# Third layer's experts: from all eight for every token to tokens packed by expert

## Chip, cores and metric

The kernel runs on one core of a Trainium2 chip. The metric is the time of one execution on the device, in microseconds, the median of several runs.

## The reference

Four transformer-like layers on 2 x 1024 tokens of width 256, all in float32, each an attention or scan part and a feed-forward part with a residual. The change is in the feed-forward part of the third layer (`L2_ffn`), on all 2048 tokens, after a normalization:

```python
E, TOP_K, I, I_SH = 8, 2, 176, 352
logits = x @ gate_w.T                                   # 2048 x 8
routing_weights, selected = top_k(softmax(logits), 2)   # then divided by their sum
out = silu(x @ shared_gate.T) * (x @ shared_up.T) @ shared_down.T      # 352 hidden rows
g = einsum('nh,eih->nei', x, expert_gate)
u = einsum('nh,eih->nei', x, expert_up)
y = einsum('nei,ehi->neh', silu(g) * u, expert_down)    # 8 experts of 176 hidden rows
out = out + einsum('neh,ne->nh', y, combine)            # combine is 0 but for the two chosen
```

## The kernel before

The program is a sequence of phases; each has its own semaphores and buffers and ends in a barrier of all engines. Inside a phase every engine has an instruction stream written out by hand, with semaphore waits; nothing reorders it. The residual `core.x` (16 tiles of 128 tokens), the normalized tokens `core.h` and their transposed copy `core.hT` stay in SBUF.

`experts2` (line 2123) is one phase. It computes all eight experts for all tokens and lets the routing weights cancel the six that aren't chosen. Shared and expert rows are stacked: 1760 hidden rows in `RC2` = 14 chunks of 128. SyncE loads the router weights `wr`, then all weights at once: `wgu`, `spread32` (a 0/1 matrix that maps experts to hidden rows), `wd`. TensorE makes the logits (line 2166). VectorE makes the softmax, the two largest and their weights, split into three bfloat16 parts in `w`, which TensorE turns (line 2188). Then for each of 4 blocks of 512 tokens and each chunk: four float32 matmuls for gate and up (line 2175; the trace shows two passes for each), and one bfloat16 matmul that spreads the weights over the hidden rows (line 2200); ScalarE does silu, VectorE multiplies twice into `hid`. The down projection (line 2209) of a block follows, 14 matmuls for each tile of 128 tokens, added to `core.x` on VectorE.

The second layer's experts (`experts1`, line 1132: 32 experts, four a token) are already built in three phases, and the change borrows their form. `route1` counts tokens by expert with matmuls and a scan, and POOL scatters rows to a DRAM buffer with 64 indirect DMAs (line 1248) while TensorE works on the shared expert (lines 1159, 1167). `expert_rows1` loads groups of four experts (`wgu` 1408 KB, `wd` 704 KB, rows `xe` 512 KB) into two slots, turns the rows (line 1422), and runs gate/up (line 1430) and down (line 1438) matmuls. `combine1` gathers the results with 64 indirect DMAs (line 1497).

Of the kernel before, what the change touches and what calls it, by code (L numbers as in the profile page):

```python
# [8 lines left out]
F32 = mybir.dt.float32  # L9
BF16 = mybir.dt.bfloat16  # L10
# [2104 lines left out]
R2 = SH2 + E2 * I2  # L2115
RM2 = [min(P, R2 - c) for c in range(0, R2, P)]
RC2 = len(RM2)
TOP2 = 2
W2 = E2 + 1
PARTS2 = 3  # L2120


def experts2(core):

    nc, ps, hT, dram = core.nc, core.ps, core.hT, core.dram
    NTB = T // BANK
    with Phase(core, "e2") as ph:
        wr = ph.sb("wr", [P, KC, E2])  # L2130
        wgu, wd = ph.sb("wgu", [P, KC, 2, R2]), ph.sb("wd", [P, RC2, H])
        spread32, spread = ph.sb("spread32", [P, R2]), ph.sb("spread", [P, R2], BF16)
# [3 lines left out]
        top, w = ph.sb("top", [P, NT, 8]), ph.sb("w", [P, NT, P])  # L2136
        rest, part = ph.sb("rest", [P, NT, E2]), ph.sb("part", [P, NT, E2], BF16)
        wT = ph.sb("wT", [P, T], BF16)
        silu, hid = ph.sb("silu", [P, 2, BANK]), ph.sb("hid", [P, 2, RC2, BANK])
        (load_r, load, const, logit, ex_in, ex_r, own_dve, w_r, turned, wT_r, gu, silu_r, wsp, hid_r, down, x_added) = (  # L2140
            ph.sem(n) for n in ("load_r", "load", "const", "logit", "ex_in", "ex", "own_dve", "w", "turned", "wT", "gu", "silu", "wsp",
                                "hid", "down", "x"))
        block = ph.block()
        each = lambda v: v.unsqueeze(2).broadcast_to([P, NT, E2])

        @block.sync
        def _(sp):
            sp.dma_start(wr[:], dram["e2_wr"]).then_inc(load_r, 16)
            for dst, name in ((wgu, "e2_wgu"), (spread32, "e2_spread"), (wd, "e2_wd")):
                sp.dma_start(dst[:], dram[name]).then_inc(load, 16)  # L2150

        @block.gpsimd
        def _(pool):
            pool.memset(prob[:], 2.0).then_inc(const, 1)
            pool.memset(w[:], 0.0).then_inc(const, 1)
            pool.wait_ge(const, 2)
            pool.memset(w[:, :, 0:1], 1.0).then_inc(const, 1)
            pool.wait_ge(load, 16 * 3)
            pool.tensor_copy(spread[:], spread32[:]).then_inc(const, 1)

        @block.tensor
        def _(pe):
            pe.wait_ge(load_r, 16)
            for t in range(NT):
                for k in range(KC):
                    last = pe.matmul(ps[:, 7, t * E2:(t + 1) * E2], hT[:, k, t * P:(t + 1) * P], wr[:, k, :], start=(k == 0),
                                     stop=(k == KC - 1))
            last.then_inc(logit, 1)

# [1555 lines left out]
```

## Time and profile before

| what | value |
|---|---|
| median of three runs | 4460.46 us (4452.94 to 4465.13) |
| the profiled execution | 4451.35 us, span 4449.6 us |
| TensorE busy | 3893.6 us, 88% of the span |
| VectorE, ScalarE, POOL busy | 52%, 39%, 28% |
| this stage, first load to the next norm | 2177.99 to 2504.66, 326.7 us |
| the second layer's experts, three phases | 1367 to about 1770 |

Times in the rows are microseconds from the start of the span. A timeline row has start, length, engine, line, operation, what it writes and reads, and in brackets the idle time before it with what ended it. SPq is SyncE's queue, PEld TensorE's weight loads. The granted clock (PEclk) is a share of TensorE's full speed: 0.5 is 1.2 GHz, 1.0 is 2.4 GHz.

### The profile page before, as it was taken

To read this page: it belongs to the slowest core of one execution; us is meant where nothing else is said; L and a number is where in the kernel's file an instruction comes from. 1 tells how busy PE (TensorE), PEld (TensorE's weight loads), DVE (VectorE), ACT (ScalarE), POOL (GpSimd) and SP (SyncE) were. 2 spreads that over 40 slices of the span, in tenths; PEclk is the share of its full clock that TensorE was granted. 3 is DMA by queue.
4 is the path that set the end of the run, shared out by engine and by line. 5 is a ranking of instruction groups with operands and counts; after the bars stand their busy time and mean duration, and the time that the engine had idled before them with its cause. 6 is when DMAs were issued, how large, how long until landed. Compare 5 with 4: busy or idle time off the path is not lost. (4 is left out here: it accounts for less than half of the span.)

```text
span 4449.6 us, 105359 instructions
## 1 busy us (share of the span) xinstructions
PE 3893.6 (88%) x45357; PEld 2419.6 (54%) x45424; DVE 2324.5 (52%) x4313; ACT 1724.7 (39%) x2719; POOL 1224.0 (28%) x1771
## 2 busy tenths in 40 slices
PE   6888769999995686799899769999999999999879
PEld 3333555555543373477655546665666665666646
DVE  4764244454456124444433247777667777677642
ACT  2345212122112010455211145656655566655532
POOL 2000120000002405321000045555554555554512
PEclk9999759999996797899899889999999999999889
DMA  1000000000003062100100000000000000000000
GB/s 51 1 1 1 30 0 27 11 1 11 11 1 110 31 191 68 41 1 1 58 0 1 6 11 9 9 9 11 10 10 9 10 9 9 9 9 9 6 15 20
DMA packets 39404, 92.00 MB, mean 21 GB/s; under 512 B 7534, under 2 KB 27791, under 8 KB 35562
## 3 DMA queue, kind: packets, MB, share of 16 engines
q1 hardware_dynamic: 28586, 69.54, 4.7%
q0 software_dynamic: 6144, 11.62, 0.9%
q8 instruction: 361, 5.91, 0.6%
q10 hardware_dynamic: 4224, 4.19, 0.3%
q14 instruction: 89, 0.73, 0.1%
HBM read 70.05 MB, written 20.45 MB: 20 GB/s over the span
## 5 line engine op out<-in xcount | busy, mean ns | idle before, releaser
L2713 PE MATMUL ps<-h_normT,h_w 128*128 128x512 f32 (+1 forms) x1008 | 423.7, 525 | 27.3 <-DVE h_xx L3300 20.3
L3234 DVE SCALAR_TENSOR_TENSOR h_cv<-h_raw,h_cw,h_cv 128x1023 f32<-128x1023 f32 (+2 forms) x288 | 391.8, 1370 | 19.7 <-ACT h_cv L3061 18.7
L3378 DVE SCALAR_TENSOR_TENSOR h_st<-h_st,d_gcs,ps 128x64 f32<-128x64 f32 x448 | 123.4, 276 | 341.9 <-PE ps L3009 341.8
L3060 ACT ACTIVATE h_raw<-ps 128x512 f32<-128x512 f32 x192 | 114.1, 594 | 401.1 <-PE ps L2713 400.3
L2713 PEld LDWEIGHTS ps<-h_normT,h_w 128*128 128x128 f32 x1008 | 164.9, 189 | 132.3 <-issue 114.6
L460 ACT ACTIVATE a_prob<-ps 128x1024 f32<-128x1024 f32 (+1 forms) x192 | 154.6, 811 | 192.7 <-PE ps L372 104.4
L944 PE MATMUL ps<-a_probT,a_v 128*128 128x512 f32 x512 | 227.8, 604 | 0.9 <-DVE a_probT L1082 0.9
L2610 POOL TENSOR_TENSOR h_gm<-h_gm,h_tmp 128x15 f32<-128x15 f32 (+7 forms) x480 | 214.7, 447 | 37.6
L2175 PE MATMUL ps<-h_normT,e_wgu 128*128 128x512 f32 (+1 forms) x448 | 203.3, 597 | 3.6 <-DMA e_wd<-in_e_wd 2.4
L1231 POOL MEMSET r_zero<- 128x2048 f32 x1 | 1.8, 1805 | 727.5 <-POOLq L54 727.5
L3009 PEld LDWEIGHTS ps<-h_st,h_mT 64*64 64x64 f32 x1792 | 90.0, 132 | 198.3 <-issue 194.1
L548 DVE TENSOR_REDUCE a_mx<-ps 128x1 f32<-128x512 f32 (+3 forms) x288 | 145.1, 549 | 70.4 <-PE ps L301 45.7
L1039 ACT ACTIVATE a_prob<-ps,a_nbias 128x1024 f32<-128x1024 f32 x64 | 71.3, 1114 | 284.5 <-DVE a_nbias L1092 284.5
L2609 POOL TENSOR_TENSOR h_tmp<-h_gm 128x15 f32<-128x15 f32 (+7 forms) x480 | 162.2, 338 | 58.6 <-DVE h_gm L3287 23.5
L2618 POOL TENSOR_TENSOR h_xT<-h_xx,d_const 32x512 f32<-32x512 f32 x64 | 66.3, 1036 | 398.6 <-DVE h_xx L3323 396.2
L2783 PE MATMUL ps<-h_wo,h_o 128*128 128x256 f32 x512 | 163.3, 434 | 6.0 <-DVE h_o L3306 3.6
L944 PEld LDWEIGHTS ps<-a_probT,a_v 128*128 128x128 f32 x512 | 98.7, 193 | 125.1 <-issue 123.9
L136 PE MATMUL ps<-ident,h_norm 128*128 128x128 f32 x256 | 45.3, 358 | 135.8 <-DVE h_norm L115 135.8
L3013 PE MATMUL ps<-h_pT,h_st 64*64 64x64 f32 x1920 | 162.0, 245 | 1.9 <-issue 1.9
L1082 DVE COPY a_probT<-ps 128x512 f32<-128x512 f32 x128 | 82.5, 685 | 154.7 <-PE ps L994 154.7
L3009 PE MATMUL ps<-h_st,h_mT 64*64 64x64 f32 x1792 | 149.3, 242 | 7.9 <-DVE h_st L3378 4.1
L2995 PE MATMUL ps<-h_ka,h_u 64*64 64x64 f32 x2048 | 144.3, 222 | 2.9 <-issue 2.8
(537 smaller groups left out, 9334.0 us busy)
## 6 DMA issues: line engine op xcount, KB each, us to landing
m_wgu<-in_m_wgu SPq DMA_DIRECT2D x8, 1408.0 KB
h_w<-in_d_w SPq DMA_DIRECT2D x48, 128.0 KB
m_wd<-in_m_wd SPq DMA_DIRECT2D x8, 704.0 KB
m_rows_in<-r_zero SPq DMA_DIRECT2D x4, 1024.0 KB
e_xe<-m_rows_in SPq DMA_DIRECT2D x8, 512.0 KB
m_rows_out<-e_y ACTq DMA_DIRECT2D x8, 512.0 KB
e_wgu<-in_e_wgu SPq DMA_DIRECT2D x1, 3520.0 KB
a_t_raw<-in_t_w SPq DMA_DIRECT2D x4, 768.0 KB
```

The source lines that it names most:

```text
L460: act.activation(prob[:, u % 3, :, c0:BANK], ps[:, SB0 + 2 * g:SB0 + 2 * g + 2, c0:BANK], ACT.Exp, scale=1.0 / float(np.sqrt(D0))).then_in ...
L548: dve.tensor_reduce(mx[:, b * NQ + qt, part, m:m + 1], ps[:, bank(), 0:k1 - k0], AX.X, ALU.max).then_inc(freed, 1)
L944: last = pe.matmul(ps[:, 6 + m, :], v[:, b * NQ + kt, m * P:(m + 1) * P], probT[:, blk % 2, kt, :], start=(kt == 0), stop=(kt == NQ - 1))
L2175: last = pe.matmul(ps[0:m, 3 * (n % 2) + s, :], wgu[:, k, s, c * P:c * P + m], hT[:, k, tok], start=(k == 0), stop=(k == KC - 1))
L2609: c.link(pool.tensor_tensor(part, column, row, ALU.mult))
L2610: c.link(pool.tensor_tensor(target, target, part, ALU.subtract))
L2713: last = pe.matmul(ps[:, PROJ[m], lo:hi], w[:, kind, k, :], hT[:, k, b * S + tb * BANK + lo:b * S + tb * BANK + hi], start=(k == 0), stop= ...
L2783: last = pe.matmul(ps[:, POUT[k], j * H:(j + 1) * H], o[:, tile * P:(tile + 1) * P], wo[:], start=True, stop=True)
L2995: last = pe.matmul(res(h, c), u_[rows(own), c, :], ka[b][rows(own), c, 1, :], start=True, stop=(c == 0), tile_position=(64 * own, 64 * (1 ...
L3009: last = pe.matmul(ps[rows(h), D3 + c % 2, 0:HALF], mT[rows(h), c, :], st[rows(h), c, :], start=False, stop=True, tile_position=(64 * h, 6 ...
L3013: last = pe.matmul(res(h, c), st[rows(h), c, :], pT[rows(h), c, :], start=False, stop=True, tile_position=(64 * h, 64 * (1 - h)))
L3234: dve.scalar_tensor_tensor(out=d, in0=raw[:, kind, 0:S - back], scalar=tap(pr, kind, TAPS3 - 1 - back), in1=d, op0=ALU.mult, op1=ALU.add). ...
```

## The change

`experts2` becomes three phases, and the expert part runs only for chosen pairs of token and expert.

`route2`: VectorE computes, for each of the two choices of every token, the row of a DRAM buffer that it goes to. The buffer is packed by expert, each expert's part rounded up to tiles of 128 rows; 39 tiles (`TILES2`) are the most that 4096 pairs can need, and all 39 are always run. VectorE also computes the expert of each tile (`eid`). SyncE zeroes the buffer (5.1 MB, four DMAs), POOL scatters the rows with 32 indirect DMAs, and the other engines do two of the four token blocks of the shared expert.

`expert_rows2`: for each tile SyncE reads its expert's number from SBUF into a register and loads the rows and that expert's weights by register address, into a ring of four slots. A round of TensorE turns the rows of one tile, multiplies the next older one by gate and up, turns the hidden rows of the one before that, and projects down the oldest.

`combine2`: POOL gathers 32 times, VectorE adds the rows with their weights, and the other two blocks of the shared expert run. Weights are laid out by expert on the host side.

```diff
+TILES2 = TOP2 * NT + E2 - 1
 def experts2(core):
+        route2(core, rows_in, wv, idx, eid, sgu, sd)
+        expert_rows2(core, rows_in, rows_out, eid)
+        combine2(core, rows_out, wv, idx, sgu, sd)
...
+def route2(core, rows_in, wv, idx, eid, sgu, sd):
...
-            for dst, name in ((wgu, "e2_wgu"), (spread32, "e2_spread"), (wd, "e2_wd")):
+            for dst, name in ((sgu, "e2_sgu"), (sd, "e2_sd")):
                 sp.dma_start(dst[:], dram[name]).then_inc(load, 16)
+            sp.wait_ge(zeroed, 1)
+            for i in range(4):
+                sp.dma_start(rows_in.rearrange("(p r) n -> p (r n)", p=P)[:, i * ZW:(i + 1) * ZW], zero[:]).then_inc(zero_put, 16)
...
+            for r in range(TOP2):
+                pool.wait_ge(routed, r + 1)
+                for t in range(NT):
+                    pool.indirect_dma_start(out=rows_in, out_offset=bass.IndirectOffsetOnAxis(ap=idx[:, r, t:t + 1], axis=0),
+                                            in_=core.h[:, t, :], in_offset=None, bounds_check=TILES2 * P - 1,
+                                            oob_is_err=False).then_inc(scattered, 16)
...
+            for c in range(SC2):
+                shared_up2(pe, core, 0, c, 0, sgu, gu, hid_r)
+            pe.wait_ge(mask_r, 1)
...
+            pe.matmul(ps[:, CNT, 0:NT * E2], before[:], flat, start=True, stop=True)
+            pe.matmul(ps[:, CNT, NT * E2:2 * NT * E2], core.ones[:], flat, start=True, stop=True).then_inc(counted, 1)
+            pe.wait_ge(routed, 1)
+            shared_down2(pe, core, 0, sd, hid, hid_r, down, x_added)
+            for c in range(SC2):
+                shared_up2(pe, core, 1, c, 1, sgu, gu, hid_r)
+            shared_down2(pe, core, 1, sd, hid, hid_r, down, x_added)
...
+def expert_rows2(core, rows_in, rows_out, eid):
+    WR = 4
...
+            for i in range(TILES2):
+                s = i % WR
+                e = sp.value_load(eid[0:1, i:i + 1], min_val=0, max_val=E2 - 1)
+                if i >= WR:
+                    sp.wait_ge(down, i - WR + 1)
+                sp.dma_start(x[:, s], xin[i]).then_inc(loaded[s], 16)
+                sp.dma_start(wgu[:, s], dram["e2_egu"][bass.ds(e, 1)].rearrange("o p k n -> (o p) k n")).then_inc(loaded[s], 16)
+                sp.dma_start(wd[:, s], dram["e2_ed"][bass.ds(e, 1)].rearrange("o p c n -> (o p) c n")).then_inc(loaded[s], 16)
...
+            def turn_in(i):
+                s = i % WR
+                pe.wait_ge(loaded[s], 48 * (i // WR + 1))
+                if i >= 2:
+                    pe.wait_ge(xT_r, i - 1)
+                for k in range(KC):
+                    last = pe.transpose(ps[:, XT + i % 2, k * P:(k + 1) * P], x[:, s, k * P:(k + 1) * P], core.ident[:])
+                last.then_inc(turned, 1)
+
+            def gate_up(i):
...
+                for k in range(KC):
+                    last = pe.matmul(ps[:, GU + i % 2, 0:2 * I2], xT[:, i % 2, k, :], wgu[:, i % WR, k, :], start=(k == 0), stop=(k == KC - 1))
...
+            def turn_hid(i):
...
+            def project_down(i):
...
+                for c, m in enumerate(IM2):
+                    last = pe.matmul(ps[:, Y + i % 2, 0:H], hidT[0:m, i % 2, c, :], wd[0:m, i % WR, c, :], start=(c == 0), stop=(c == IC2E - 1))
+                last.then_inc(down, 1)
+
+            turn_in(0)
+            for i in range(TILES2 + 2):
+                if i + 1 < TILES2:
+                    turn_in(i + 1)
+                if i < TILES2:
+                    gate_up(i)
+                if 0 <= i - 1 < TILES2:
+                    turn_hid(i - 1)
+                if 0 <= i - 2 < TILES2:
+                    project_down(i - 2)
...
+                    act.activation(silu[:, i % 2, :], ps[:, GU + i % 2, 0:I2], ACT.Silu).then_inc(silu_r, 1)
...
+                    act.activation(y[:, n % WR, :], ps[:, Y + n % 2, 0:H], ACT.Copy).then_inc(y_r, 1)
+                    act.wait_ge(y_r, n + 1)
+                    act.dma_start(yout[n], y[:, n % WR]).then_inc(stored[n % WR], 16)
...
+def combine2(core, rows_out, wv, idx, sgu, sd):
...
+            for t in range(NT):
+                for r in range(TOP2):
+                    pool.indirect_dma_start(out=row[:, TOP2 * t + r, :], out_offset=None, in_=rows_out,
+                                            in_offset=bass.IndirectOffsetOnAxis(ap=idx[:, r, t:t + 1], axis=0),
+                                            bounds_check=TILES2 * P - 1, oob_is_err=False).then_inc(fetched[t], 16)
...
+            inner(0, 0)
+            add_rows(0)
+            inner(0, 1)
+            add_rows(1)
...
```

SyncE's queue in this stage before: the whole of its work is four loads at the start. (`e_wgu` and `e_wd` hold all 1760 rows.)

```order
91 L2146 UNCONDITIONAL_BRANCH [waits barrier_Pool_Activation_PE_DVE_SP_release]
92 L2148 DMA e_wr<-in_e_wr 128x16
93 L2150 DMA e_wgu<-in_e_wgu 128x7040
94 L2150 DMA e_spread<-in_e_spread 128x1760
95 L2150 DMA e_wd<-in_e_wd 128x3584
```

The same queue now, in the phase of the tiles, at tiles 3 and 4. Semaphores are named by their number's first user in the program; `a0_smax` is `down` here. TENSOR_LOAD reads the expert's number, ISA rows compute addresses.

```order
120 L2358 TENSOR_LOAD e_eid
121 L2358 ISA x2
122 L2361 DMA g_x<-e_rows_in 128x256
123 L2362 ISA
124 L2362 DMA g_wgu<-in_e_egu 128x704
125 L2363 ISA
126 L2363 DMA g_wd<-in_e_ed 128x512
127 L2358 TENSOR_LOAD e_eid
128 L2358 ISA x2
129 L2361 DMA g_x<-e_rows_in 128x256 [waits a0_smax]
```

From tile 4 on the first of the three DMAs waits for `down`, and the other two are queued behind it.

TensorE before, after the weights are turned: chunk after chunk, each waiting only for a buffer freed two chunks earlier.

```order
2825 L2175 MATMUL ps<-h_normT,e_wgu 128x512 [waits a0_vproj]
2826 L2175 MATMUL ps<-h_normT,e_wgu 128x512 x3
2827 L2200 MATMUL ps<-e_wT,e_spread 128x512
2828 L2175 MATMUL ps<-h_normT,e_wgu 128x512 [waits a0_vproj]
2829 L2175 MATMUL ps<-h_normT,e_wgu 128x512 x3
```

TensorE now, from turn_in(3) in round 2 to turn_in(4) in round 3. Line 2373 is turn_in, 2381 gate_up, 2389 turn_hid, 2397 project_down. `ln0_rstd` stands for `loaded[3]`, `init_loaded` for `loaded[0]`.

```order
2846 L2373 MATMUL ps<-ident,g_x 128x128 [waits a0_qr,ln0_rstd]
2847 L2373 MATMUL ps<-ident,g_x 128x128
2848 L2381 MATMUL ps<-g_wgu,g_xT 128x352 [waits a0_kzd,a0_qr]
2849 L2381 MATMUL ps<-g_wgu,g_xT 128x352
2850 L2389 MATMUL ps<-ident,g_hid 128x128 [waits a0_kzd]
2851 L2389 MATMUL ps<-ident,g_hid 48x128
2852 L2397 MATMUL ps<-g_wd,g_hidT 128x256 [waits a0_vd]
2853 L2397 MATMUL ps<-g_wd,g_hidT 128x256
2854 L2373 MATMUL ps<-ident,g_x 128x128 [waits a0_qr,init_loaded]
```

The second row of line 2397 is the one that counts up `down`; the row behind it is the first that needs the slot's next load.

## Rows read from the trace of the kernel before

**Rows 1.** The page, part 1: busy time, share of the span, instructions

```profile
PE 3893.6 (88%) x45357; PEld 2419.6 (54%) x45424; DVE 2324.5 (52%) x4313; ACT 1724.7 (39%) x2719; POOL 1224.0 (28%) x1771
```

**Rows 2.** Windows of the stage: length, busy by engine, PEclk, DMA share, GB/s

```profile
2178.00:2196.00 18.00, 13.82 (x64) 13.73 (x64) 1.85 (x12) 2.88 (x3) 2.18 (x3) 0.54 0.87 353
2196.00:2304.00 108.00, 105.88 (x262) 47.20 (x268) 43.78 (x113) 18.19 (x31) 1.65 (x1) 0.98 0.00 0
2304.00:2504.00 200.00, 199.06 (x696) 129.96 (x700) 46.88 (x74) 17.31 (x29) 0.00 (x0) 1.00 0.00 1
```

**Rows 3.** Timeline of all engines at the stage's edges

```profile
2177.99 0.33 SPq L2148 DMA_DIRECT2D e_wr<-in_e_wr  x1
...
2179.78 13.82 PE L2166 MATMUL ps<-e_wr,h_normT 128*128 128x8 f32 x64 [3.16 <-DMA e_wr<-in_e_wr]
...
2196.05 8.99 PE L2175 MATMUL ps<-h_normT,e_wgu 128*128 128x512 f32 x16 [2.44 <-DMA e_wd<-in_e_wd]
...
2201.65 0.60 ACT L2223 ACTIVATE e_silu<-ps 128x512 f32<-128x512 f32 x1 [5.74 <-PE ps L2175]
...
2504.66 5.33 DVE L107 BATCH_NORM_STATS2 ln_stats<-x_resid 128x6 f32<-128x256 f32 x16 [0.82 <-PEq L54]
```

**Rows 4.** Timeline of the second layer's routing, from the counts to the first scatter

```profile
1413.95 3.34 DVE L1343 TENSOR_TENSOR r_offs<-ps,r_offs 128x32 f32<-128x32 f32 x15
...
1421.41 0.17 DVE L1356 CAST r_sidx<-r_got 128x16 int32<-128x16 f32 x1
...
1422.62 1.23 POOL L1248 DMA_INDIRECT m_rows_in<-h_norm,r_sidx  x1 [41.16 <-issue]
```

**Rows 5.** Line 1248 (the 64 scatters): ns min/median/max, first and last start

```profile
L1248 POOL DMA_INDIRECT m_rows_in<-h_norm,r_sidx x64: 971/976/1226, 1422.6 to 1504.7; - x64
```

**Rows 6.** Timeline of SyncE's loads in the second layer's expert phase

```profile
1543.36 1.12 SPq L1404 DMA_DIRECT2D e_xe<-m_rows_in  x2
1561.14 0.36 SPq L1409 DMA_DIRECT2D m_wgu<-in_m_wgu  x1
...
1562.21 0.38 SPq L1411 DMA_DIRECT2D e_xe<-m_rows_in  x1
...
1588.66 0.34 SPq L1409 DMA_DIRECT2D m_wgu<-in_m_wgu  x1
```

**Rows 7.** Timeline of TensorE in the same phase

```profile
1547.47 1.76 PE L1422 MATMUL ps<-ident,e_xe 128*128 128x128 f32 x7 [6.19 <-DMA e_xe<-m_rows_in]
...
1569.25 3.62 PE L1438 MATMUL ps<-m_wd,e_hid 88*128 88x256 f32 x16
1575.22 1.97 PE L1422 MATMUL ps<-ident,e_xe 128*128 128x128 f32 x8 [2.35 <-DMA e_xe<-m_rows_in]
...
1584.88 3.62 PE L1438 MATMUL ps<-m_wd,e_hid 88*128 88x256 f32 x16
1588.34 1.04 PE L1422 MATMUL ps<-ident,e_xe 128*128 128x128 f32 x8
```

**Rows 8.** Windows of the same phase's start: length, busy by engine, PEclk, DMA share, GB/s

```profile
1544.00:1547.50 3.50, 0.03 (x1) 0.03 (x1) 0.00 (x0) 0.00 (x0) 0.00 (x0) 0.57 0.80 249
1547.50:1551.00 3.50, 3.50 (x16) 3.17 (x17) 1.39 (x2) 0.00 (x0) 0.00 (x0) 0.50 0.17 55
1551.00:1561.00 10.00, 10.00 (x76) 9.53 (x76) 1.68 (x4) 1.52 (x4) 0.00 (x0) 0.99 0.00 0
```

**Rows 9.** Timeline of TensorE under and after the second layer's last scatters

```profile
1507.76 1.01 PE L1159 MATMUL ps<-h_normT,m_sgu 128*128 128x512 f32 x1 [1.79 <-issue]
1510.55 17.33 PE L1159 MATMUL ps<-h_normT,m_sgu 128*128 128x512 f32 x36 [1.78 <-issue]
```

**Rows 10.** Timeline between the second layer's expert and combine phases

```profile
1652.56 1.02 ACT L1456 ACTIVATE e_y<-ps 128x1024 f32<-128x1024 f32 x1 [3.08 <-PE ps L1438]
...
1657.64 22.41 PE L1159 MATMUL ps<-h_normT,m_sgu 128*128 128x512 f32 x48 [5.12 <-PEq L54]
...
1659.78 1.01 POOL L1497 DMA_INDIRECT c_row<-m_rows_out,m_gidx  x1 [0.30 <-issue]
```

More of the change, by code:

```diff
@@ new lines, in shared_up2, with shared_down2 @@
+def shared_up2(pe, core, b, c, tb, sgu, gu, hid_r):
+    n, m = b * SC2 + c, SM2[c]
+    if n >= 3:
+        pe.wait_ge(hid_r, n - 2)
+    for s in range(2):
+        for k in range(KC):
+            last = pe.matmul(core.ps[0:m, 2 * (n % 3) + s, :], sgu[:, k, s, c * P:c * P + m], core.hT[:, k, tb * BANK:(tb + 1) * BANK],
+                             start=(k == 0), stop=(k == KC - 1))
+    last.then_inc(gu, 1)
+def shared_down2(pe, core, b, sd, hid, hid_r, down, x_added):
+    pe.wait_ge(hid_r, (b + 1) * SC2)
+    for j in range(4):
+        if b >= 1 and j % 2 == 0:
+            pe.wait_ge(x_added, 4 * b + j - 2)
+        for c in range(SC2):
+            last = pe.matmul(core.ps[:, 6 + j // 2, (j % 2) * H:(j % 2 + 1) * H], hid[0:SM2[c], b, c, j * P:(j + 1) * P], sd[0:SM2[c], c, :],
+                             start=(c == 0), stop=(c == SC2 - 1))
+        if j % 2:
+            last.then_inc(down, 1)
@@ new lines, in _ @@
+            own.link(dve.tensor_tensor(cnt[:], cnt[:], each(two_t[:]), ALU.subtract))
+            own.link(dve.tensor_tensor(cnt[:], cnt[:], mask[:], ALU.mult))
+            dve.wait_ge(counted, 1)
+            tot = ps[:, CNT, NT * E2:2 * NT * E2].rearrange("p (t e) -> p t e", e=E2)
+            own.link(dve.memset(offs[:, 0, :], 0.0))
+            for t in range(1, NT + 1):
+                own.link(dve.tensor_tensor(offs[:, t, :], tot[:, t - 1, :], offs[:, t - 1, :], ALU.add))
+            own.link(dve.tensor_tensor(pos[:], ps[:, CNT, 0:NT * E2].rearrange("p (t e) -> p t e", e=E2), offs[:, 0:NT, :], ALU.add))
@@ new lines, in _ @@
+            own.link(dve.tensor_tensor(ex[:], ex[:], each(linv[:]), ALU.mult))
+            for r in range(TOP2):
+                chosen(wv[:, r, :], r, ex[:])
+            for b in range(2):
+                for c in range(SC2):
+                    n, m = b * SC2 + c, SM2[c]
+                    dve.wait_ge(silu_r, n + 1)
+                    dve.tensor_tensor(hid[0:m, b, c, :], ps[0:m, 2 * (n % 3) + 1, :], silu[0:m, n % 3, :], ALU.mult).then_inc(hid_r, 1)
+                for j in range(4):
+                    t = 4 * b + j
+                    dve.wait_ge(down, 2 * b + j // 2 + 1)
+                    dve.tensor_tensor(core.x[:, t, :], ps[:, 6 + j // 2, (j % 2) * H:(j % 2 + 1) * H], core.x[:, t, :],
+                                      ALU.add).then_inc(x_added, 1)
```

335 lines of the change are left out of this document (219 added, 116 removed).

## The prediction

> **What bounds the kernel now.** I read the page's first part, then the stage of the third layer's experts by stretches, then its edges in the timeline. TensorE is busy for 88% of the whole span [rows 1]; in the stage itself it is busy 105.88 of 108 us and 199.06 of 200 us in the two stretches after routing, at a granted clock of 0.98 and 1.00, while DMA moves nothing and VectorE idles more than half [rows 2]. So the stage is TensorE's own work at full clock. It begins when SyncE issues its first load at 2177.99 and ends where the next layer's norm begins at 2504.66: 326.7 us [rows 3]. Nothing else of the program is edited, so the sum is: new length of this stage minus 326.7.
>
> The edit cuts that work. Before, every token goes through 1760 hidden rows; after, through 352 shared rows and 39 tiles of 128 packed rows. If TensorE stayed the bound this would pay. The question is what the other engines and the loads do, and the second layer's experts (lines 1183 to 1536) are built the same way, so their rows price nearly every new step.
>
> **Part 1, routing (`route2`).** Logits cost what they do now: 13.8 us from 2179.78, to 2193.6 [rows 2, 3]. Then three shared chunks run. Now the first chunk of eight 512-column passes needs 5.6 us (2196.05 to 2201.65), as the clock is still low (0.54 before it) [rows 2, 3]. At full clock sixteen 256-column passes, as many columns, took 3.6 us [rows 7], 3.4 without the last one's drain. So 5.6 + 3.4 + 3.4 puts the counting matmuls at 2206.1, and 0.6 us later VectorE has its counts. The second layer's chain from there to its first index cast took from 1413.95 to 1421.58, 7.6 us on rows of 512 elements [rows 4]; here the rows have 128, and I take 5.8 us: 2212.5. The other routing arithmetic lies beside the shared chunks or beside the scatters. POOL's first scatter followed the cast by 1.2 us [rows 4]. There are 32 scatters where the second layer has 64; those 64 started between 1422.6 and 1504.7, 1.30 us apart, 0.98 us each [rows 5]: 31 x 1.30 + 0.98 = 41.3 us, ending at 2255.0. Landing costs about 1.8 us, as the 8 KB load's (2177.99 to 2179.78) [rows 3], and the phase's end 1.5 us: **2258.3, or 80.3 us**. What is left of the shared work (a down projection of 5.2 us, three chunks of 10.3, 5.2 again: 21 us) fits under the 41 us of scatters. Zeroing 5.1 MB of the row buffer is over by then: the same stretch now moves 353 GB/s for 18 us [rows 2]. One thing can break the cover: under the second layer's scatters TensorE fell to one matmul per 2.8 us until they were over, with nothing else for it to wait for (1.01 us busy, 1.79 idle by "issue" each, ending in the burst at 1510.55) [rows 9]. I add nothing here and up to 12 us in the range.
>
> **Part 2, the expert tiles (`expert_rows2`).** This decides. Follow one ring slot. SyncE loads tile i only when `down` has counted tile i-4. TensorE runs, in order: turn_in(i+1), gate_up(i), turn_hid(i-1), project_down(i-2). So project_down(0) is the last thing of round 2, and turn_in(4), which needs the load that project_down(0) has just released, is the first thing of round 3. **Four slots are held by a pipeline four deep: no load is ever ahead.** TensorE executes in order, so everything of a round is queued behind the landing, and for tiles 4 to 38, 35 times, the period is a whole load plus a whole round.
>
> *The load.* 128 x (256 + 704 + 512) x 4 bytes = 0.754 MB in three DMAs. Two landings of the second layer's experts bracket it: 0.524 MB issued at 1543.36 let TensorE start at 1547.47 (4.11 us), and 2.687 MB issued at 1561.14 at 1575.22 (14.08 us) [rows 6, 7]; 8 KB took 1.79 us [rows 3]. The line from 8 KB to either gives 4.4 and 4.6 us per MB, so 1.79 + 0.754 x 4.5 = 5.2 us. From the end of a down projection to SyncE's issue lie 0.16 us (1584.88 + 3.62 to 1588.66) [rows 6, 7]. So **5.3 us**. Bounds: at the rate of the stage's own big load, 353 GB/s [rows 2], it is 1.79 + 2.1 + 0.16 = 4.1 us; the third issue comes 1.07 us after the first (1561.14 to 1562.21) [rows 6], which gives no less than 3.8; the previous tile's 0.131 MB store in the way makes it 5.9.
>
> *The round.* Full clock: eight transposes took 1.04 us, so 2 + 2 cost at most 0.52; sixteen 256-column passes 3.62 us, so four cost 0.90 and four of 352 columns 1.24 [rows 7]. Sum 2.66 us. At low clock transposes took 1.97 us for the same eight [rows 7]; everything doubled is 5.3 us. Which clock? After TensorE's waits the clock was 0.57 (1544 to 1547.5), stayed at 0.50, which is 1.2 GHz, for the first 3.5 us of work, and was 0.99 after that [rows 8]. Each round here follows 5 us without a matmul, so it starts low: 3.5 us low, and the remaining third at full speed, 3.5 + 1.8 / 2 = 4.4, say **4.5 us**. The bounds are 2.7 (full clock throughout) and 5.3 (never back).
>
> Period 5.3 + 4.5 = **9.8 us**, 35 times: 343 us. In front stand the first four loads, 5.2 + 3 x 3.3 us (0.754 MB x 4.4), and most of a round behind them: 19 us. Behind stand three rounds without loads, about 7 us, and the last store: in the second layer 5.1 us from the end of the last down projection (1652.5) to the next phase's start at 1657.64 [rows 10]. **Together 374 us.** ScalarE's and VectorE's work, about 1.5 us a tile each, lies inside the load and costs nothing; so do SyncE's register load and two address computations per tile, since they run before `down` arrives, except for those of the second and third DMA, which are in the 1.07 us above.
>
> The Trainium skill ("DMA: Bandwidth & Descriptors", "Anatomy of one DMA") fits a transfer as 2.0 us plus bytes at 436 GB/s, measured on another issuing path. It would make the load 3.9 us and the total 49 us shorter. The second layer's two landings were slower than that, 4.4 and 4.6 us per MB against 2.3, so the sum goes by them.
>
> **Part 3, gathering (`combine2`).** 32 gathers, each 1.00 us busy and 0.30 idle as in the second layer [rows 10]: 0.8 + 41.3, then 2 us for the last landing and adds, 1.2 for the barrier: 45 us. The other half of the shared work, 31 us, runs beside it. VectorE's adds come in strict order with the shared blocks, so a starved TensorE shows here; I add 5 us: **50 us**.
>
> **Sum.** 80.3 + 374 + 50 = 504.3 us, plus 0.8 us of barriers, against 326.7: **+178 us**. The profiled execution took 4451.35 us, so 4630; it lies 9.1 us below the median of 4460.46, so against the median **4640 us**, rounded.
>
> **Rivals.**
> 1. *Same mechanism, quick landings and early clock.* Load 4.1 us, round 4.0: 35 x 1.7 = 60 us less, 4580; at the bounds of both (3.8 + 2.7) 4525. For: the queue that moved 353 GB/s. Against: both landings of tiles with 1 KB rows.
> 2. *Same mechanism, clock never back and TensorE starved.* Load 5.9, round 5.3: +49 us, plus 12 for starving: 4701. For: rounds of 5 us barely outlast the 3.5 us that the clock took to return, and rows 9.
> 3. *Faster: the ring does run ahead.* If loads streamed, the period would be the larger of TensorE's 2.66 us and the bytes: 0.885 MB in and out at the second layer's 13.1 us for 3.2 MB (1575.22 to 1588.34) [rows 7], 3.6 us. Then 35 x 6.2 = 217 us less: 4423. It decides the sign below a period of 4.7 us (9.8 - 178 / 35). Against it stands the order of the code: even the 8 KB landing (1.79 us) with a full-clock round gives 4.5 us, which only just gets there, and a tile's load is 90 times that size. The Trainium skill ("Trainium Kernel Development and Optimization", "Best Practices") says to double-buffer so that DMA overlaps compute; four slots look like twice that, and by that rule this rival would be the forecast. Whether slots run ahead depends on when they are freed, which the code order shows.
> 4. *The change doesn't cut the work:* all 39 tiles always run, and their rounds sum to 104 us at full clock against 305 now (105.88 + 199.06) [rows 2], so it does.
>
> **Chances.** Forecast with a period of 8.8 to 10.8 us: 0.72. Rival 1: 0.14. Rival 2: 0.09. Rival 3: 0.04. Something that cancels to within 0.3% (about what a measurement of this kernel can tell from no change): 0.01. Faster 0.04, same 0.01, slower 0.95. The range takes in rival 1 down to a period of 7.0 us and rival 2 whole: 4540 to 4705.
>
> **What the profile after should show.** SyncE issuing three DMAs every 9.8 us, each first one about 0.2 us after the line-2397 matmuls end; TensorE idle before line 2373, released by DMA, 35 times about 5.3 us; granted clock in these stretches between 0.5 and 0.8; DMA share near 0.3, about 90 GB/s; scatters 1.28 to 1.30 us apart. Wrong would be: TensorE's waits before line 2373 under 2 us (rival 3), or waits on ScalarE or VectorE inside a round.

## The result and the profile after

The changed kernel takes **4643.48 us** (median of four runs, 4640.71 to 4651.48), the kernel before in the same comparison 4461.24 us (4452.94 to 4465.13): ratio **1.042, 95% interval 1.040 to 1.044**, 182 us slower. The forecast was 4640 us. The profiled execution took 4644.92 us, its span is 4642.8.

TensorE's line on the page answers to [rows 1], and the one group that the change added to the page's list of the costliest points at the cause:

```profile
PE 3857.5 (83%) x45064; PEld 2393.6 (52%) x45120; DVE 2320.7 (50%) x4434; ACT 1723.5 (37%) x2749; POOL 1288.3 (28%) x1838
...
L2373 PE MATMUL ps<-ident,g_x 128*128 128x128 f32 x78 | 26.5, 442 | 172.7 <-DMA g_wd<-in_e_ed 172.7
```

TensorE's busy time fell only from 3893.6 to 3857.5 us, since much of the smaller work is done at half clock, and 172.7 us of idle time stand before line 2373, the transposes that wait for a tile's load. The edges of the three phases, from the timelines of SyncE, POOL and VectorE, answer to [rows 3]:

```profile
2177.29 0.33 SPq L2203 DMA_DIRECT2D r_wr<-in_e_wr  x1
...
2269.32 0.33 SPq L2361 DMA_DIRECT2D g_x<-e_rows_in  x1
...
2640.23 1.04 POOL L2474 DMA_INDIRECT c2m_row<-e_rows_out,e_idx  x1 [387.12 <-SPq L51]
...
2703.48 1.73 DVE L107 BATCH_NORM_STATS2 ln_stats<-x_resid 128x6 f32<-128x256 f32 x5 [0.88 <-PEq L54]
```

The last phase's first matmul stands at 2639.5, 0.7 us before the first gather. So:

| part | predicted | measured |
|---|---|---|
| routing | 80.3 | 92.0 |
| tile phase | 374 | 370.2 |
| gathering | 50 | 64.0 |
| stage | 505 | 526.2 |
| stage, before | 326.7 | 326.7 |

The stage grew by 199.5 us, the span by 193.2: what stands ahead of the stage was 0.7 us shorter and what follows it 5.6 us shorter in this execution. The medians differ by 182.2.

The windows (length, busy time of each engine, granted clock, DMA share, GB/s), to be read against [rows 2]:

```profile
2212.00:2253.00 41.00, 18.04 (x48) 10.48 (x48) 8.71 (x23) 1.19 (x2) 31.34 (x32) 0.71 0.28 100
...
2284.90:2619.40 334.50, 175.44 (x408) 96.39 (x408) 39.31 (x136) 23.82 (x69) 0.00 (x0) 0.60 0.27 90
```

In the second row's 334.5 us the ring goes round 34 times, from SyncE's fifth load to its last: 9.84 us a tile. TensorE works 175.44 us of it, 5.16 a tile, at a mean clock of 0.60, and DMA is 27% busy: **neither is a limit, they take turns.** The table of waits for that stretch (engine, line waited at, releaser: us in total, times, longest) has the other 4.68 us:

```profile
PE ps L2373 <- DMA g_wd<-in_e_ed: 159.1, 34, 5.7
```

One turn in the timeline of all engines:

```profile
2289.26 0.69 PE L2373 MATMUL ps<-ident,g_x 128*128 128x128 f32 x2 [4.43 <-DMA g_wd<-in_e_ed]
...
2289.74 2.55 PE L2381 MATMUL ps<-g_wgu,g_xT 128*128 128x352 f32 x4
...
2292.08 0.63 PE L2389 MATMUL ps<-ident,g_hid 128*128 128x128 f32 x2
...
2292.51 2.21 PE L2397 MATMUL ps<-g_wd,g_hidT 128*128 128x256 f32 x4
...
2294.75 0.33 SPq L2361 DMA_DIRECT2D g_x<-e_rows_in  x1
...
2299.30 0.69 PE L2373 MATMUL ps<-ident,g_x 128*128 128x128 f32 x2 [4.59 <-DMA g_wd<-in_e_ed]
```

The down projection ends at 2292.51 + 2.21 = 2294.72; SyncE issues the load of the tile four further on 0.03 us later; TensorE's next instruction needs just that load. Windows of one such turn show the clock (the seventh figure is PEclk):

```profile
2324.00:2325.50 1.50, 0.00 (x0) 0.00 (x0) 0.00 (x0) 0.00 (x0) 0.00 (x0) 0.99 0.92 282
2325.50:2327.70 2.20, 0.00 (x0) 0.00 (x0) 0.00 (x0) 0.00 (x0) 0.00 (x0) 0.50 0.56 197
2327.70:2329.70 2.00, 1.97 (x5) 1.48 (x6) 0.42 (x1) 0.00 (x0) 0.00 (x0) 0.50 0.00 0
2329.70:2331.70 2.00, 2.00 (x6) 0.96 (x5) 0.46 (x2) 0.32 (x1) 0.00 (x0) 0.50 0.00 0
2331.70:2333.20 1.50, 1.11 (x3) 0.44 (x2) 0.36 (x2) 0.35 (x1) 0.00 (x0) 0.80 0.02 5
```

In this turn it drops to 1.2 GHz halfway through the wait and comes back to 2.4 GHz about when the round is over. The turns are not alike. In 14 of the 34 it stays at 0.50 from the start of the round to the end of the wait, as in the turn shown before:

```profile
2289.26:2299.30 10.04, 5.46 (x12) 2.90 (x12) 1.15 (x4) 0.70 (x2) 0.00 (x0) 0.50 0.28 88
```

In the other 20 it comes back between 2.7 us into the round and the round's end. Windows laid on every round and every wait give a mean of 0.54 in the rounds and of 0.67 in the waits, so most of the little time at the higher clock goes to an idle engine.

What the sum left out lies in the two phases with indirect DMAs. In the first of the two windows, under the scatters, TensorE works only 18.04 of 41 us. ScalarE's silu steps in the routing phase (timeline, with idle time and releaser in brackets), and the matmuls behind them (`remote`: the profile names no engine of this core as releaser):

```profile
2235.03 0.60 ACT L2171 ACTIVATE r_silu<-ps 128x512 f32<-128x512 f32 x1 [29.70 <-remote]
2249.17 0.60 ACT L2171 ACTIVATE r_silu<-ps 128x512 f32<-128x512 f32 x1 [13.54 <-remote]
2257.63 0.59 ACT L2171 ACTIVATE r_silu<-ps 96x512 f32<-96x512 f32 x1 [7.86 <-remote]
...
2258.99 7.92 PE L2158 MATMUL ps<-e_sd,r_hid 128*128 128x256 f32 x24 [22.58 <-DVE r_hid L2327]
```

Such steps follow each other 3.44 us apart when nothing disturbs them (0.60 + 2.84), and the first is due near 2229.4, 3.4 us after the second block's matmuls begin at 2225.95. Here, under the scatters (32 of them, started between 2212.2 and 2252.1), it is 5.7 us late, and they stand 14.1 and 8.5 us apart, so the last down projection begins at 2259 and ends after the scatters that should have covered it. In the last phase the same happens under the gathers: its last down projection waits 18.81 us and starts at 2687.71.

### The profile page after: what moved, and what is told of

It is laid out like the page before. It is cut to its first block and busy times, and to the rows that moved or that the text cites. A ratio compares the mean times of both kernels' runs of the same rounds, so it can differ in the third digit from the quotient of the medians.

```text
span 4642.8 us, 105738 instructions
## 1 busy us (share of the span) xinstructions
PE 3857.5 (83%) x45064; PEld 2393.6 (52%) x45120; DVE 2320.7 (50%) x4434; ACT 1723.5 (37%) x2749; POOL 1288.3 (28%) x1838
## 5 line engine op out<-in xcount | busy, mean ns | idle before, releaser
L2373 PE MATMUL ps<-ident,g_x 128*128 128x128 f32 x78 | 26.5, 442 | 172.7 <-DMA g_wd<-in_e_ed 172.7
```

## Experiments

Times are medians unless one time is said, and ratios are to runs of the kernel before on the same chip. Its median there was 4453.25 us for the first four kernels and 4451.74 for the two after them, against 4461.24 in the comparison above, so a difference to the changed kernel's 4643.48 carries an uncertainty of some 10 us; the periods in the traces do not.

### One more slot, and twice the slots

The ring's size is one number, in `expert_rows2`.

```diff
-    WR = 4
+    WR = 5
```

> The changed kernel with five slots in the ring of tiles instead of four. Theory (a load is released at the end of a round and, with four slots, needed at the start of the next; with n slots the period is (load + round) / (n - 3), down to the larger of the round and the bytes): one load is ahead, the period falls from 9.84 us to (5.1 + 2.7) / 2 to (5.1 + 4.5) / 2 = 3.9 to 4.8 us, TensorE's waits before line 2373 to 1 or 2 us each, the clock back near 1.0; 35 x 5.0 to 5.9 = 175 to 207 us less than 4643, so 4436 to 4468. Rival (the loads' rate is the bound, 0.885 MB at the 90 GB/s that the stretch shows): the period stays 9.8 us and the time 4643.

Measured: 4441.63 us, ratio to the kernel before 0.998 (0.996 to 1.000). The time is in the range that was expected. From SyncE's sixth load (2283.65) to its last (2421.82) the period is 4.19 us on average, where it was 9.84. The rounds vary: most run at full clock in 2.9 us, some at a mean clock near 0.63 in 4.5 us. Timeline of TensorE:

```profile
2333.96 0.44 PE L2373 MATMUL ps<-ident,g_x 128*128 128x128 f32 x2 [1.41 <-DMA g_wd<-in_e_ed]
...
2337.10 0.44 PE L2373 MATMUL ps<-ident,g_x 128*128 128x128 f32 x2 [0.24 <-DMA g_wd<-in_e_ed]
```

```diff
-    WR = 4
+    WR = 8
```

> The changed kernel with eight slots. Theory: four loads ahead, so the period is the larger of a full-clock round, 2.7 us, and the bytes, 0.885 MB at 245 GB/s, 3.6 us; 35 x 6.2 = 217 us less than 4643, so 4426, and little better than five slots (0 to 40 us). DMA share 0.8 or more, 240 GB/s or more in the stretch. Rival (rate bound at 90 GB/s): 4643.

Measured: **4395.68 us** (4389.94 to 4398.91), ratio 0.988 (0.986 to 0.990), the fastest of all and 248 us under the changed kernel. One round of TensorE and the start of the next, and a window over the loaded part of the tile phase, from SyncE's ninth load to its last:

```profile
2301.70 0.44 PE L2373 MATMUL ps<-ident,g_x 128*128 128x128 f32 x2
2301.98 1.35 PE L2381 MATMUL ps<-g_wgu,g_xT 128*128 128x352 f32 x4
2303.16 0.38 PE L2389 MATMUL ps<-ident,g_hid 128*128 128x128 f32 x2
2303.38 1.22 PE L2397 MATMUL ps<-g_wd,g_hidT 128*128 128x256 f32 x4
2304.54 0.44 PE L2373 MATMUL ps<-ident,g_x 128*128 128x128 f32 x2
```

```profile
2283.00:2366.00 83.00, 83.00 (x354) 49.62 (x352) 33.53 (x116) 20.65 (x59) 0.00 (x0) 1.00 0.95 323
```

No bracket stands behind any row: TensorE never waits here, its clock is 1.00, and the period is its own 2.84 us. The stage took 269.9 us (2176.14 to 2446.05) against 326.7: 57 us less, and the medians differ by 57.6. So the slots are the cause, and the price of the missing one is the largest term of all. The expectation for eight slots was 30 us too high: it took 3.6 us a tile as the bytes' limit, and they fit under 2.84 us. But they only just fit: the 16 DMA engines are busy for 95% of the window, at 323 GB/s, so a shorter round of TensorE would gain little.

### The same four slots, another order

A slot is freed by the down projection of tile i-2. Here that comes first in a round instead of last, and the transposes that need the next load come last.

```diff
             turn_in(0)
             for i in range(TILES2 + 2):
-                if i + 1 < TILES2:
-                    turn_in(i + 1)
+                if 0 <= i - 2 < TILES2:
+                    project_down(i - 2)
                 if i < TILES2:
                     gate_up(i)
                 if 0 <= i - 1 < TILES2:
                     turn_hid(i - 1)
-                if 0 <= i - 2 < TILES2:
-                    project_down(i - 2)
+                if i + 1 < TILES2:
+                    turn_in(i + 1)
```

> The changed kernel with four slots, but TensorE's round in the order project_down(i-2), gate_up(i), turn_hid(i-1), turn_in(i+1): the same work, the slot is freed before gate_up and turn_hid instead of right before the wait. Theory (it is the place of the release that counts): period = down + load + turn_in = 0.9 + 5.1 + 0.3 at full clock to 1.8 + 5.1 + 0.5 at low clock, 6.3 to 7.4 us; 35 x 2.4 to 3.5 = 85 to 120 us less, so 4523 to 4558. Rival (the sum of load and round is fixed by something else): 4643.

Measured: 4457.22 us, ratio 1.002 (1.001 to 1.004); the period is 4.29 us from 2311.8 on. Four rounds before that (2279.2 to 2307.3) take 7.02 us each, with the clock at 0.50, so the mean over all loads behind the fourth is 4.59. The lowest time that was expected, 4523, was 66 us too high. Timeline of TensorE:

```profile
2330.56 1.32 PE L2397 MATMUL ps<-g_wd,g_hidT 128*128 128x256 f32 x4 [1.15 <-DVE g_hidT L2453]
...
2334.85 1.33 PE L2397 MATMUL ps<-g_wd,g_hidT 128*128 128x256 f32 x4 [1.15 <-DVE g_hidT L2453]
```

The wait for the load is gone altogether. `project_down(i-2)`, at the start of round i, frees the slot of tile i+2, which is wanted by `turn_in(i+2)`, at the end of round i+1: nearly two rounds later. The expectation had counted less than one. What comes late now is VectorE's copy of the turned hidden rows (line 2453), which the down projection follows directly, and that puts 1.15 us of idle time into each period. So 186 us can be had back without a byte of memory.

### What the clock costs

Nine float32 matmuls of 256 columns, whose result nobody reads, ahead of TensorE's wait for a load (tiles 4 to 38).

```diff
                 s = i % WR
+                if i >= WR:
+                    for f in range(9):
+                        pe.matmul(ps[:, XT + i % 2, H:2 * H], core.ident[:], core.h[:, f, :], start=True, stop=True)
                 pe.wait_ge(loaded[s], 48 * (i // WR + 1))
```

> The changed kernel with work added, none taken away: before each wait for a load (tiles 4 to 38) nine float32 matmuls of 256 columns into an unused half of a PSUM bank, 3.9 us at full clock, whose results nobody reads. Theory (the low clock in each round comes from TensorE's idle time in the load): the clock in the stretch rises from 0.60 to near 1.0, the round falls from 4.5 to 2.7 us, period 5.1 + 2.7 = 7.8 to 8.0 us; 35 x 1.9 = 65 us less, 4578, though there is more work. Rival (the round is long for another reason, as latencies between the engines): the period stays at 9.8 or grows.

Measured: 4561.06 us, 82 us *less* than the changed kernel with 145 us more work (35 x 4.15) on the same engine. Timeline of TensorE:

```profile
2330.39 4.15 PE L2371 MATMUL ps<-h_norm,ident 128*128 128x256 f32 x18
2335.09 0.44 PE L2376 MATMUL ps<-ident,g_x 128*128 128x128 f32 x2 [0.55 <-DMA g_wd<-in_e_ed]
2335.36 1.35 PE L2384 MATMUL ps<-g_wgu,g_xT 128*128 128x352 f32 x4
```

Line 2384 is the old 2381: 1.35 us instead of 2.55, and the clock stays at 1.00. The period is 7.56 us on average over the 34 (SyncE's fifth load at 2292.58, its last at 2549.49) instead of 9.84, so the low clock costs 2.3 us a round; the load stays in the path, 4.15 + 0.55 = 4.7 us in the rows shown.

### What the weights' part of the load costs

Here the weights are loaded for the first four tiles only, and later tiles take what lies in their slot; only the rows are loaded anew, and TensorE waits for that one DMA (its changed wait is not shown).

```diff
+                if i >= WR:
+                    continue
                 sp.dma_start(wgu[:, s], dram["e2_egu"][bass.ds(e, 1)]...).then_inc(loaded[s], 16)
                 sp.dma_start(wd[:, s], dram["e2_ed"][bass.ds(e, 1)]...).then_inc(loaded[s], 16)
```

> The changed kernel, but the expert weights are loaded for the first four tiles only; from tile 4 on SyncE loads just the packed rows, so the later tiles multiply by stale weights. Load 0.131 MB instead of 0.754 MB, one DMA instead of three. Theory (load = 1.8 us + 4.5 us per MB): load 1.8 + 0.6 + 0.16 = 2.5 us instead of 5.1; round 2.7 to 4.5 us as the clock goes; period 5.2 to 7.0 us, so 100 to 162 us less than 4643: 4481 to 4543. Rival (a fixed cost makes the load, not its bytes): load 4.5 us or more, 4620.

Measured: 4538.67 us, ratio 1.017 (1.008 to 1.027), within the range that was expected. Timeline of TensorE (line 2375 is the old 2373):

```profile
2305.82 0.44 PE L2375 MATMUL ps<-ident,g_x 128*128 128x128 f32 x2 [2.04 <-DMA g_x<-e_rows_in]
```

With 0.131 MB instead of 0.754 the wait is 2.0 us instead of 4.7: 2.7 us for 0.623 MB, 4.3 us per MB, near what the two landings of the second layer had. That isn't bytes alone, for two DMAs went with them, and the last of three is issued 1.03 us after the first (2284.86 and 2285.89 in the profile after); how the 2.7 us divide is not shown. A load of a sixth of the bytes, put in the path, still leaves the kernel slower than before. **What decides is the turn-taking; the bytes set what a turn costs.**

### Why the shared blocks fall behind under the indirect DMAs

POOL waits until the shared blocks are done before it scatters.

```diff
             pool.wait_ge(zero_put, 16 * 4)
+            pool.wait_ge(x_added, 8)
```

> The changed kernel, with POOL's 32 scatters held back until the two shared blocks of the routing phase have been added. Theory (it is POOL's indirect DMAs that starve the other engines: ScalarE's gaps of 13 us before line 2171, VectorE's before line 2327, TensorE's 22.6 us): without scatters beside them the shared blocks end near 2243 instead of 2267, no gap over 3 us before these lines; the scatters then take 41 us alone, the phase ends near 2286 instead of 2269, +17 us: 4660. Rival (the gaps belong to the shared block's own waits): they stay, the phase ends near 2310, +40 us: 4683.

Measured: 4676.01 us, ratio 1.048 (1.038 to 1.058). With no scatter beside them, ScalarE's steps stand in their row (timeline):

```profile
2237.15 0.60 ACT L2171 ACTIVATE r_silu<-ps 128x512 f32<-128x512 f32 x1 [23.14 <-PE ps L2146]
2240.58 0.60 ACT L2171 ACTIVATE r_silu<-ps 128x512 f32<-128x512 f32 x1 [2.84 <-PE ps L2146]
```

In the kernel of the section above, on the same chip, they are late as in the changed kernel (2233.43, 2246.78, 2255.92). So the indirect DMAs are what delays them. But giving up the overlap costs more than the delay: the routing phase takes 114.6 us (SyncE at 2184.55 and 2299.19) against 92.0, 23 us more where 17 were expected. The rest of the 33 us between the medians is not from the edit alone, since in the profiled execution the stage begins 7.3 us later and what follows it is 9.6 us longer than in the changed kernel's, while the other two phases are 8 us shorter; the cause of these is not shown.

To see what is late, instructions or semaphores, runs that wait for nothing inside were put beside these late scatters: 80 activations, 60 reductions on VectorE, 40 matmuls of 512 columns.

```diff
+            act.wait_ge(x_added, 8)
+            for n in range(80):
+                act.activation(pa[:, n, :], core.hT[:, 0, (n % 8) * 256:(n % 8 + 1) * 256], ACT.Silu)
```

> The kernel with the scatters held back until the routing phase's shared blocks are added, and, beside the scatters, work added whose results nobody reads: 80 silu of 256 columns on ScalarE (0.4 us each), 60 reductions of 512 elements on VectorE (0.7 us), 40 float32 matmuls of 512 columns on TensorE (0.86 us each in two passes), each engine's in one run with no semaphore between them. Theory A (under POOL's indirect DMAs the other engines get their instructions late): gaps of 1 us and more without a semaphore appear inside these runs on one or more engines, and they take longer than 32, 42 and 34 us. Theory B (it is the semaphores that arrive late): the runs go through without gaps, and only work that waits for another engine is slow.

Measured: 4689.66 us (one time). Timelines of ScalarE, VectorE and TensorE; rows without gaps between instructions are drawn together:

```profile
2243.90 16.36 ACT L2267 ACTIVATE r_pa<-h_normT 128x256 f32<-128x256 f32 x53 [7.06 <-DVE x_resid L2339]
...
2263.28 0.42 ACT L2267 ACTIVATE r_pa<-h_normT 128x256 f32<-128x256 f32 x1 [1.01 <-issue]
```

```profile
2243.79 35.68 DVE L2342 TENSOR_REDUCE r_pd<-h_normT 128x1 f32<-128x512 f32 x60
```

```profile
2243.92 28.59 PE L2258 MATMUL ps<-h_norm,ident 128*128 128x512 f32 x66 [0.84 <-DVE x_resid L2339]
...
2282.23 1.01 PE L2258 MATMUL ps<-h_norm,ident 128*128 128x512 f32 x1 [1.79 <-issue]
```

No semaphore stands between these instructions, and still ScalarE comes to start one only every 1.40 us and TensorE one pass every 2.80, the spacing of [rows 9], until the scatters are over; then both run without gaps. So it is not semaphores that are late in these runs, but the instructions; why they are is not shown. The second probe asks whether the first 53, 60 and 66 are a number or a time, with 160, 200 and 120 shorter ones (here VectorE's, against the first probe):

```diff
-            for n in range(60):
-                dve.tensor_reduce(pd[:, n:n + 1], core.hT[:, 0, 0:BANK], AX.X, ALU.max)
+            for n in range(200):
+                dve.tensor_reduce(pd[:, n:n + 1], core.hT[:, 0, 0:P], AX.X, ALU.max)
```

> As the kernel with the late scatters, with longer runs of shorter instructions beside them, none of which waits for anything inside its run: 160 silu of 64 columns on ScalarE, 200 reductions of 128 elements on VectorE, 120 matmuls of 128 columns (240 passes) on TensorE. In the first probe ScalarE ran 53 activations in 16.4 us without a gap and then one every 1.40 us until the scatters were over; TensorE ran 66 passes in 28.6 us and then one every 2.80 us; VectorE's 60 had no gap at all (35.7 us). Theory A (count: an engine has some 50 to 66 instructions at hand when the scatters start, and what comes after arrives late): ScalarE's first gap comes after about 53 again, so after some 8 us instead of 16; TensorE's after about 66 passes, some 10 us; VectorE, spared before because its run was short, falls into gaps as well after some 60, about 10 us after its start, and its 200 take until the scatters end. Theory B (time: it takes 16 and 28 us of scatters until the engines are hit): gaps begin at the same times as before, after far more instructions, most of them done by then. Theory C (VectorE is exempt): its 200 show no gap while the others do. The whole program comes out near 4690 to 4700 us, as the first probe did.

Measured: 4691.84 us (one time). Timelines of ScalarE, VectorE and TensorE:

```profile
2243.58 7.59 ACT L2267 ACTIVATE r_pa<-h_normT 128x64 f32<-128x64 f32 x51 [7.06 <-DVE x_resid L2339]
2251.55 0.40 ACT L2267 ACTIVATE r_pa<-h_normT 128x64 f32<-128x64 f32 x2 [0.38 <-issue]
```

```profile
2243.47 11.68 DVE L2342 TENSOR_REDUCE r_pd<-h_normT 128x1 f32<-128x128 f32 x60
2255.83 0.48 DVE L2342 TENSOR_REDUCE r_pd<-h_normT 128x1 f32<-128x128 f32 x2 [0.68 <-issue]
```

```profile
2243.60 7.19 PE L2258 MATMUL ps<-h_norm,ident 128*128 128x128 f32 x62 [0.85 <-DVE x_resid L2339]
2251.55 0.40 PE L2258 MATMUL ps<-h_norm,ident 128*128 128x128 f32 x2 [0.76 <-issue]
```

A number: 51 to 66 instructions (of TensorE, passes) run freely, whether they last 7 us or 28, and VectorE, which its short run had spared, falls into gaps after exactly 60. Theory A holds for these runs.

### The delay comes and goes with the chip or the session

The next kernel was meant to show the same inside the changed kernel, by 8 activations ahead of each of the second block's silu steps.

```diff
             act.wait_ge(hid_r, n - 2)
+            for r in range(8):
+                act.activation(silu[0:m, n, 64 * r:64 * r + 64], core.hT[0:m, 0, 0:64], ACT.Silu)
```

> The changed kernel; in both phases with shared blocks, each of the second block's three silu steps on ScalarE is preceded, behind its waits, by 8 activations of 64 columns that wait for nothing. In the changed kernel the first of these silu steps ran 5.7 us late in the routing phase (2235.03, where 2229.4 is due), the second 10.7 later than its place in the row, the third 5.0. Theory A (late instructions, ScalarE's store of instructions empty or soon used up): inside each run of 8 there are gaps of about 1.1 us, as in the probes (one activation every 1.40 us), or they begin after a few of the 8; the three runs cost some 3 x 8 x 1.4 = 34 us minus what the shortage cost anyway, and the routing phase ends some 10 to 15 us later than 2269, or at the latest soon after the last scatter. Theory B (the semaphore arrives late, instructions are at hand): the 8 stand without a gap (about 1.2 us together), right before the late silu, in all three places, and the phase ends within 4 us of 2269.

Measured: 4593.4 us (one time), 50 us *below* the changed kernel, and the kernel before took 4436.99 beside it. Neither theory had this: no step was late anywhere, nor in the second layer's phases, which the edit does not touch. Three more runs on one chip, the changed kernel itself among them, and one with 48 activations where ScalarE waits anyway:

```diff
+            for r in range(48):
+                act.activation(spare[:, r, :], core.hT[:, 0, 0:64], ACT.Silu)
             for i in range(TILES2 + 2):
```

> The changed kernel once more, unedited, beside the next two on one chip. The kernel with the 8 activations ahead of each silu of the second shared block had come out 50 us faster than the changed kernel (4593.4 against 4643.5): no silu was late in either phase with shared blocks, and the second layer's shared blocks, whose code it does not touch, were not starved either (phase start 1630.8 instead of 1661.8). Theory C (chip or execution: in some, the engines are not starved beside the indirect transfers, whatever the kernel): this run comes out near 4593 too, or varies between 4593 and 4643 from run to run. Theory L (layout: it depends on the lengths of the instruction streams and on where they lie): this run gives 4640 to 4652 again.

> The kernel with three runs of 8 activations in each of the two phases, unedited, on the chip of the run before it. Theory L: 4590 to 4600 again, with the silu steps on time. Theory C: the same as the run of the changed kernel on this chip, within some 10 us.

> The changed kernel with the same number of additional activations (48 of 64 columns), all at the start of the tile phase on ScalarE, where it waits 15 us for TensorE anyway; the shared blocks' code is as in the changed kernel. Theory L (the lengths of the streams matter, not the activations' place): 4590 to 4600, with the second layer's shared blocks spared as well. Theory C: as the changed kernel on this chip. Theory P (the activations help by their place, by keeping ScalarE supplied): as the changed kernel here, and the kernel before it in this call faster; but that would not explain the second layer.

| kernel, on that chip | median | ratio to before |
|---|---|---|
| before | 4418.37 (4409.55 to 4423.01) | |
| changed, unedited | 4597.88 (4593.45 to 4606.32) | 1.042 (1.039 to 1.044) |
| 3 x 8 activations in each phase | 4595.81 (4588.59 to 4605.67) | 1.040 (1.038 to 1.042) |
| 48 activations elsewhere | 4590.39 (4578.64 to 4602.12) | 1.039 (1.036 to 1.042) |

Before came out 43 us and the unedited changed kernel 46 us below their medians in the first comparison, and the two edits stand within 8 us of the unedited kernel: theory C, and theory L falls. Edges and ScalarE's steps of the changed kernel there (timelines of SyncE, ScalarE, POOL, VectorE):

```profile
2134.68 0.33 SPq L2203 DMA_DIRECT2D r_wr<-in_e_wr  x1
...
2185.42 0.60 ACT L2171 ACTIVATE r_silu<-ps 128x512 f32<-128x512 f32 x1 [24.25 <-PE ps L2146]
2188.85 0.60 ACT L2171 ACTIVATE r_silu<-ps 128x512 f32<-128x512 f32 x1 [2.84 <-PE ps L2146]
...
2214.75 0.32 SPq L2361 DMA_DIRECT2D g_x<-e_rows_in  x1
...
2585.53 1.04 POOL L2474 DMA_INDIRECT c2m_row<-e_rows_out,e_idx  x1 [376.65 <-SPq L51]
...
2631.68 5.32 DVE L107 BATCH_NORM_STATS2 ln_stats<-x_resid 128x6 f32<-128x256 f32 x16 [1.17 <-PEq L54]
```

The same program, the same 32 scatters 1.28 us apart, and no late step. Routing takes 80.1 us instead of 92.0, gathering 46.9 instead of 64.0, so the stage takes 497.0 us instead of 526.2. It also begins 42.6 us earlier, mostly because the second layer's shared blocks are no longer starved: its expert phase begins at 1512.8 instead of 1550.7. Not all of this reaches the end, since the part of the program behind the stage is longer there, at a lower granted clock; here are windows of it, the first in the profile after, the second on this chip:

```profile
2703.40:4642.00 1938.60, 1770.50 (x35482) 1143.86 (x35522) 1254.83 (x1977) 1064.20 (x1695) 925.62 (x1440) 0.95 0.03 10
```

```profile
2631.60:4592.00 1960.40, 1796.09 (x35522) 1157.21 (x35522) 1253.59 (x1977) 1065.01 (x1695) 925.22 (x1440) 0.93 0.03 10
```

In the four profiled executions without the delay this part took 1953 to 1960 us, in the other ten 1939 to 1950; why is not shown.

Open is what differs between the chips: these runs and that of the first 8-activation kernel were on two chips, the others on four or more, and no chip on record appears twice, so it may also be something of the session. Open, too, is why in the changed kernel ScalarE is late after only a few instructions, where the probes found more than 50 at hand; the run made to show it met a chip without the delay, so that it is the same lateness in the changed kernel is likely but not shown.

## Why the prediction was right, step by step

**The mechanism is the one of the forecast.** "Four slots are held by a pipeline four deep" shows in the load issued 0.03 us after the down projection and in 34 waits of 4.68 us. One slot more, or the freeing step put first with four slots, takes 202 and 186 us away; eight slots make a period of TensorE's own length. Rival 3 is what the change would have been with slots that run ahead, and the order of the code was reason enough to give it 0.04. Its 4423 us was 27 higher than the kernel with eight slots, for its byte limit of 3.6 us a tile came from the second layer's period, which cannot have been that limit; eight slots ran at 2.84. The forecast's full-clock round, 2.66 us, was 0.18 short of that.

**The period's two terms were off in opposite directions.** Predicted 5.3 + 4.5, measured 4.7 + 5.16. The load came 0.6 us quicker; the issue took no 0.16 us but 0.03, and the rest is landing. The slope of 4.5 us per MB was near the 4.3 of the experiment on the rows, issues included, so what stands ahead of the slope was taken too long. The Trainium skill ("DMA: Bandwidth & Descriptors", "Anatomy of one DMA") fits a DMA that POOL issues by 2.0 us plus bytes at 436 GB/s: an estimate of 3.7 us for 0.754 MB, 3.9 with the forecast's issue. The 4.7 us that were measured here, for three DMAs of SyncE, do not agree with it, and it lay further off than the forecast's 5.3. The round was longer since the clock did not come back 3.5 us into it as in [rows 8]: in 14 of 34 turns it never did, and the mean over the rounds was 0.54. "The remaining third at full speed", which took the clock to return, is the step of the sum that failed; 5.16 is close to the 5.3 of rival 2, whose clock was right. The two errors over 35 rounds are -21 and +23 us, and that they cancel is luck. What the tile phase came out below 374, at 370.2, is from its ends: 15.5 us ahead of the first period (19 predicted) and 10.2 behind the last (12 predicted).

**Starving was sized too low.** The forecast added nothing in routing, "up to 12 in the range", and 5 in gathering. Measured were 11.7 and 14 us more than the two terms. Routing's own arithmetic was right: the first scatter at 2212.2 where 2213.7 was forecast, the last one done at 2253.1 where 2255.0 was; and on the chip without the delay the phases took 80.1 and 46.9 us against 80.3 and 50 (45 without the 5 for starving). The step that failed was the cover: 21 us of shared work under 41 us of scatters looks like twice the room needed, but [rows 9] had shown TensorE at a small fraction of its pace there. The forecast named TensorE; it was ScalarE that stood late first, with VectorE and TensorE behind it.

**Why the total hit all the same.** This is luck. The stage's growth was 199.5 us against the 178 of the sum; 0.7 us ahead of the stage and 5.6 behind it, which the edit does not touch, were given back, and the forecast then added 9.1 us to go from the profiled execution of before to its median, while the profiled execution of after lies 1.4 us *above* its own. So the sum was 21 us short, starving made 26 of that with the tile phase giving 4 back, and differences between executions hid most of it.

## To carry to other kernels

Count the slots of a ring against the stages that hold them in TensorE's order, and look at which instruction frees a slot and which one next needs it; if they are neighbours, the whole load stands in the path, whatever the ring's size suggests, and moving the freeing step to the round's start was worth nearly as much as a slot (186 us against 202). A wait of 4.7 us a round cost half as much again, 2.3 us, since the clock falls in it and most of the work behind it runs at 1.2 GHz. Work placed under a train of indirect DMAs may get its instructions late, and two kernels should be compared on one chip and in one session: the medians of one and the same kernel differ here by 43 and 46 us of some 4500, a quarter of what the change cost.

## What the runs showed of the hardware

- In two probes beside indirect DMAs of POOL, ScalarE, VectorE and TensorE ran 51 to 66 instructions without a gap and then settled to one every 1.40 us (TensorE one pass every 2.80), until the last indirect DMA was done. Such lateness stood in the traces from some chips and not in those from two others, with the same program: 4643.5 against 4597.9 us for the changed kernel, 4461.2 against 4418.4 for the one before.
- Nine matmuls whose result nobody reads, ahead of each wait, 145 us of work in all, made the program 82 us faster: the clock stayed at 1.00, and gate and up took 1.35 us instead of 2.55.
- Three DMAs of 0.754 MB together landed 4.7 us after the slot came free when each tile's load stood alone, while the same loads kept up 2.84 us a tile, 323 GB/s with the stores and the DMA engines 95% busy, as soon as eight slots let them run ahead.
